# Coupling pass of a graph network kernel: radial part beside the vector part in a 57 column message, sums over four tiles at once

## The chip, the cores and the metric

The kernel runs on one core of a Trainium2 chip (trn2). The metric is the device time of one execution in microseconds. The engines of the core are TensorE (PE in the profile; PEld is its weight load), VectorE (DVE), ScalarE (ACT), GpSimd (POOL) and SyncE (SP); each works through its own instruction stream in order, and they meet at semaphores.

## The reference, cut to what matters

The reference applies four graph layers to 12,500 nodes of 32 values and 400,000 edges, with a residual and a layer norm after each. The change touches the third layer only, a coupling with spherical harmonics. Its features are 8 scalars and 8 vectors of 3 components:

```python
R = jax.nn.relu(abs_distances[:, None] @ w1 + b1) @ w2 + b2      # (E, 384)
Y = spherical_harmonics(rel_vec)
Fj = features[src]
for i, (mo, lo) in enumerate(RS):                # RS = [(8, 0), (8, 1)]
    acc = jnp.zeros((E, mo, 2 * lo + 1))
    for j, (mi, li) in enumerate(RS):
        ...
        acc = acc + _NORM[i] * jnp.einsum('euv,ef,evi,ofi->euo', Rb[..., k], Yf, Fb, C)
    msg_blocks.append(acc.reshape(E, -1))
msg = jnp.concatenate(msg_blocks, axis=-1)       # (E, 32)
out = out.at[dst].add(msg)
```

The edges are sorted by `dst`. The coupling is worked out in the kernel as 40 sums of 16 terms for each edge: 8 for the scalar part of the message, 8 for a coefficient that multiplies the unit vector of the edge (the radial part), and 24 for the vector part. The vector output of an edge is the vector part plus the unit vector times its coefficient.

## The kernel before, in words

**Tiles and steps.** The edges, padded to groups, lie in tiles of 128, one edge on each partition. A step takes 8 tiles (`TPS`), in four groups of two tiles (`GPS`, `TILES_PER_GROUP`); the edges of a group go to nodes of one window of 128. The coupling pass has 416 steps: 104 iterations (`ITERS`) of 4 slots (`SLOTS`).

**What each engine does for step n** (all `radial_...` functions):

- GpSimd (`radial_gather`): 8 indirect DMAs fetch the features of the source nodes (L779). Three tensor operations, the "geometry" (L819, L820, L824), make the cross products for a later step; they stand between the first four and the last four gathers. In 96 of the 104 iterations (`LATE_ROUNDS`, 384 steps) two further indirect DMAs (L760) fetch edge records that only the last iterations will use: the late records.
- ScalarE (`radial_round`) copies unit vectors and features into place (L1077 to L1082), applies the bias and relu to the hidden layer (L1088), makes the one-hot matrices that select a node (L1094, L1099), and copies the sums of each group back into the accumulator (`keep_sums`, L1057).
- TensorE (`radial_step`, L1396) makes for each pair p = 0 to 3 of tiles two matmuls of 384 columns, the radial weights (L1405), called R0 to R3 below. They go to banks 1 and 2 for even p and to 3 and 4 for odd p. Between them stand the hidden layer of the next step (L1371, L1377) and the four group sums of the step before (`radial_sums`: L1390 loads the accumulator, L1392 adds two tiles). The order is fixed: R0, L1371, R1, sums 0, R2, half of the hidden layer, sums 1, R3, sums 2, the other half, sums 3.
- VectorE (`radial_step`, L2453) multiplies the radial weights of pair p by the features into `prod` (L2467 for the first 256 columns of both tiles, L2472 for the rest of each tile) and sums 16 terms at a time into `red` (L2478).

**Semaphores around the change.** `r_ready` tells VectorE that the pair's matmuls are done; `r_used`, raised by the second L2472 of pair p, lets TensorE overwrite the banks two pairs later: R2 waits for pair 0, R3 for pair 1, R0 of the next step for pair 2, R1 for pair 3. `hid_ready` (ScalarE) gates R0 as well. `msg_ready`, raised by L2485, lets TensorE start sums 0 of that step and ScalarE start its copies for the step after the next. `geo_ops` makes VectorE wait for the geometry of GpSimd, `geo_ready` makes GpSimd wait for the copies of ScalarE.

**The end of a step on VectorE.** After the four sums L2481 forms the radial part (24 columns) in a tile of its own, and L2485 adds it to columns 16 to 39 of `red`. Then L2457 and L2461 start the next step.

`prod` has two halves, each of two tiles, so pair p overwrites what pair p-2 left. The names `C2` (41), `red`, `radial` and `prod` are those that the change touches.

## Time and profile before

| what | value |
|---|---|
| median of 3 runs | 20600.07 us (20592.81 to 20604.26) |
| the profiled execution's own time | 20595.7 us |
| its span, first to last instruction | 20593.9 us |
| coupling pass in the span, first to last multiplication and sum of VectorE | 10738.7 to 16783.6 us |
| VectorE busy over the span | 17281.9 us (84%) |
| GpSimd busy over the span | 13246.4 us (64%) |
| TensorE matmul busy over the span | 9779.6 us (47%) |
| mean granted TensorE clock | 0.67 |

The time is that of the whole execution; the span lies 1.8 us below it. The passes follow each other with little overlap, so a change within the coupling pass is to be read from the rows of that pass. Rows of one timeline give the start, the duration, engine, line, operation, the tiles written and read, the count merged into the row, and in brackets the idle time before it with what ended it.

### The profile page before, as it was taken

The page shows a single profiled execution, that of the slowest core. Times are in us where ns is not written, and L with a number is a line of the kernel's source. Part 1 is how long each engine was busy: PE and PEld are TensorE (multiplying, and loading weights), DVE is VectorE, ACT ScalarE, POOL GpSimd, SP SyncE. Part 2 cuts the span into 40 slices and gives each one's busy share as a digit, 9 for nine tenths or more (in the row PEclk, how much of TensorE's full clock was granted, in tenths as well). Part 3 has the DMA queues.
Part 4 walks back from the last instruction along what each step waited for, and adds up shares of the span by engine and source line. Part 5 has one row for each costly group of instructions (what it writes and reads, how often), then busy time and mean ns, then how long its engine had stood idle before and what let it go on. Part 6 is the DMA issues. An engine that isn't in the chain of part 4 may idle for free.

```text
span 20593.9 us, 293981 instructions
## 1 busy us (share of the span) xinstructions
PE 9779.6 (47%) x63545; PEld 7463.1 (36%) x63546; DVE 17281.9 (84%) x25284; ACT 5966.3 (29%) x13901; POOL 13246.4 (64%) x14067
## 2 busy tenths in 40 slices
PE   0114010110016777653348777777777765336432
PEld 0114010100015666643235555555555544225322
DVE  9989999999997888787659999999999986664666
ACT  0000333333322222230004444454545445004300
POOL 0058777777777777735757777777777731770376
PEclk9655555555558888755558888888888875555555
DMA  1033444444412112174331111111111147336534
GB/s 18 0 54 24 30 35 31 33 31 32 33 22 45 36 36 36 34 242 124 84 52 12 12 12 12 12 12 12 12 12 12 12 89 230 79 77 162 181 79 68
DMA packets 1751558, 1095.98 MB, mean 53 GB/s; under 512 B 1217323, under 2 KB 1658124, under 8 KB 1750028
## 3 DMA queue, kind: packets, MB, share of 16 engines
q0 software_dynamic: 454272, 412.11, 18.2%
q1 hardware_dynamic: 1089532, 417.46, 8.2%
q10 hardware_dynamic: 207632, 265.14, 4.1%
q14 instruction: 88, 0.72, 0.0%
q8 instruction: 34, 0.56, 0.0%
HBM read 700.94 MB, written 391.12 MB: 53 GB/s over the span
## 4 chain that ended last, share of the span: by engine, by line
DVE 43%; DVEq 20%; issue 12%; DMA 10%; PE 10%; POOL 3%; ACT 1%; ACTq 0%; POOLq 0%; SPq 0%
DVEq L2477 11%; DMA srcs<-spread,nbx 9%; DVE arena L1750 7%; DVE arena L1749 6%; DVE srcs L2472 6%; POOL srcs L801 3%; DVE red L2478 3%; PE banks L1264 2%; DVEq L2205 2%; PE banks L1347 2%; DVE arena L1722 2%; DVE arena L2173 2%; DVE arena L1567 2%; PE banks L1405 1%; PE banks L1193 1%
## 5 line engine op out<-in xcount | busy, mean ns | idle before, releaser
L779 POOL DMA_INDIRECT gat<-tab,nbr x3328 | 3509.4, 1054 | 2151.3 <-DMA nbr<-nbr_src 1137.2
L801 POOL DMA_INDIRECT srcs<-spread,nbx x2808 | 2654.9, 945 | 2713.5 <-DMA nbx<-from_src 1375.3
L779 POOL DMA_INDIRECT gat<-tab,pay x3328 | 3176.8, 955 | 1078.4 <-issue 854.3
L1405 PE MATMUL banks<-w2rows,dsts 128*128 128x384 f32 x6656 | 3177.9, 613 | 894.1 <-DVE srcs L2472 700.2
L745 POOL DMA_INDIRECT pay<-records,nbr x2560 | 2489.7, 973 | 797.7 <-issue 780.0
L2478 DVE TENSOR_REDUCE red<-srcs 128x80 f32<-128x1280 f32 x1664 | 2474.6, 1487 | 151.4
L2173 DVE TENSOR_TENSOR arena<-arena,banks 128x96 f32 (+2 forms) x4472 | 1210.4, 271 | 1474.0 <-PE banks L1264 890.6
L1193 PE MATMUL banks<-ident,arena 128*128 128x128 f32 x2240 | 426.3, 376 | 4231.5 <-DVE arena L1750 2810.2
L1264 PE MATMUL banks<-srcs,hot 128*128 128x96 bf16 (+1 forms) x11232 | 1148.5, 278 | 2482.7 <-DMA srcs<-spread,nbx 2364.0
L906 ACT COPY banks<-arena 128x1024 f32<-128x1024 f32 (+1 forms) x1508 | 1324.5, 879 | 3299.6 <-DVE arena L1750 1275.6
L1405 PEld LDWEIGHTS banks<-w2rows,dsts 128*128 128x128 f32 x6656 | 1359.9, 227 | 1735.0 <-DVE srcs L2472 849.2
L1193 PEld LDWEIGHTS banks<-ident,arena 128*128 128x128 f32 x2240 | 401.4, 203 | 4257.7 <-DVE arena L1750 2820.3
L1264 PEld LDWEIGHTS banks<-srcs,hot 128*128 128x128 bf16 x11232 | 883.1, 135 | 2748.1 <-issue 1567.9
L2472 DVE TENSOR_TENSOR srcs<-banks,g_v 128x384 f32<-128x384 f32 x3328 | 1685.0, 548 | 0.0
L1749 DVE TENSOR_TENSOR arena<-banks,arena 128x1024 f32<-128x1024 f32 (+1 forms) x1508 | 1544.0, 1024 | 22.8 <-ACT banks L906 22.8
L1750 DVE TENSOR_TENSOR arena<-banks,arena 128x1024 f32<-128x1024 f32 (+1 forms) x1508 | 1544.1, 1024 | 0.0
L1347 PE MATMUL banks<-arena,hotT 128*128 x11232 | 1078.8, 282 | 829.8 <-DVE hotT L2260 576.6
L2260 DVE TENSOR_SCALAR hotT<-dsts,lanes 128x1024 bf16<-128x1024 uint8 x1404 | 1026.8, 757 | 469.5 <-PE banks L1347 467.1
L1347 PEld LDWEIGHTS banks<-arena,hotT 128*128 128x128 bf16 x11232 | 894.4, 141 | 1014.0 <-issue 1009.6
L2467 DVE TENSOR_TENSOR srcs<-banks,g_s 128x512 f32<-128x512 f32 x1664 | 1137.6, 684 | 142.1 <-issue 96.6
L2162 DVE TENSOR_TENSOR hot<-banks,key_dst 128x1024 bf16<-128x1024 f32 x936 | 1141.4, 1220 | 53.1 <-issue 52.9
L1392 PE MATMUL banks<-red,hot 128*128 128x41 f32 x6656 | 1162.5, 307 | 0.0
(394 smaller groups left out, 20741.4 us busy)
## 6 DMA issues: line engine op xcount, KB each, us to landing
spread<-srcs SPq DMA_DIRECT2D x936, 192.0 KB
dsts<-key_rows SPq DMA_DIRECT2D x234, 512.0 KB, 4.1
spread<-srcs ACTq DMA_DIRECT2D x468, 204.0 KB
staged<-gat SPq DMA_DIRECT2D x416, 148.0 KB, 1.8
gat<-staged ACTq DMA_DIRECT2D x416, 148.0 KB
dsts<-key_rows ACTq DMA_DIRECT2D x117, 512.0 KB, 4.5
gat<-tab,nbr POOLq DMA_INDIRECT x3328
gat<-tab,pay POOLq DMA_INDIRECT x3328
```

The lines of the kernel that those rows point to most:

```text
L745: pool.indirect_dma_start(out=pay[:, s, t, :], out_offset=None, in_=records, in_offset=bass.IndirectOffsetOnAxis(ap=nbr[:, s, t:t + 1], ax ...
L779: pool.indirect_dma_start(out=gatv(s, GC[pas])[:, t, :], out_offset=None, in_=TAB[pas], in_offset=bass.IndirectOffsetOnAxis(ap=row, axis=0 ...
L801: pool.indirect_dma_start(out=chunk_rows(s, c)[:, q, :], out_offset=None, in_=rows, in_offset=bass.IndirectOffsetOnAxis(ap=nbx[:, r, s * X ...
L1264: last = t_.matmul(where(q), hots[:, t, :], rows(t), start=(h == 0), stop=(h == tiles - 1))
L1347: last = t_.matmul(bank[2 * (s % 2) + q][:, j * c3:(j + 1) * c3], hotT_row[s % 2][:, q * XGROUP + j:(q + 1) * XGROUP:CHUNK_EDGES], tabs[:, ...
L1405: last = t_.matmul(bank[1 + 2 * (p % 2) + h][:, 0:384], hid_rows[:, s % 2, 2 * p + h, :], w2rows[:, :], start=True, stop=True)
L1749: v.tensor_tensor(b[:, d, e, :, :, :], held, a[:, d, 1, :, :, :], ALU.min)
L1750: last = v.tensor_tensor(b[:, d, 1 - e, :, :, :], held, a[:, d, 1, :, :, :], ALU.max)
L2173: last = v.tensor_tensor(dst, dst, where(q), ALU.add)
L2472: last = v.tensor_tensor(prod[:, pb, h, 16:40, :].rearrange("p (u o) k -> p u o k", o=3), bank[lo + h][:, 256:384].rearrange("p (u a k) -> ...
L2477: dve.drain()
L2478: v.tensor_reduce(red[:, b, t0:t0 + 2, 0:40], prod[:, pb, :, :, :], AX.X, ALU.add)
```

## The change

Each message gets 57 columns in place of 41. `red` is 65 columns wide: 0 to 7 hold the radial coefficients, 8 to 15 the scalar part, 16 to 39 the vector part, 40 a one that counts the edges, and 41 to 64 the radial part. TensorE sends columns 8 to 64. The radial part is written there directly and is no longer added on VectorE; it is added once, per node, after the pass. `prod` is one buffer of four tiles, and the sum over 16 terms is taken after every second pair, over four tiles. The two blocks of `w2rows` are swapped to match, and the late records of GpSimd stay as they were.

```diff
-C2 = 41
+C2 = 57
+CR = 65
...
-        red = sb("red", [P, 2, TPS, C2])
+        red = sb("red", [P, 2, TPS, CR])
...
-        prod = srcs[:, 0:4 * 640].bitcast(F32).rearrange("p (b t r k) -> p b t r k", b=2, t=2, k=16)
+        prod = srcs[:, 0:4 * 640].bitcast(F32).rearrange("p (t r k) -> p t r k", t=TPS // 2, k=16)
...
-        radial = sb("radial", [P, TPS, 24])
...
-                    last = t_.matmul(where, hot[:, s % 2, t, :], red[:, s % 2, t, :], start=False,
+                    last = t_.matmul(where, hot[:, s % 2, t, :], red[:, s % 2, t, 8:CR], start=False,
...
-                    t0, pb, lo = 2 * p, p % 2, 1 + 2 * (p % 2)
+                    t0, f0, lo = 2 * p, 2 * (p % 2), 1 + 2 * (p % 2)
                     dve.wait_ge(r_ready, n * (TPS // 2) + (p + 1))
-                    v.tensor_tensor(prod[:, pb, :, 0:16, :],
+                    v.tensor_tensor(prod[:, f0:f0 + 2, 0:16, :],
...
                     last.then_inc(r_used, 1)
-                    dve.drain()
-                    v.tensor_reduce(red[:, b, t0:t0 + 2, 0:40], prod[:, pb, :, :, :], AX.X, ALU.add)
-                dve.drain()
-
-                v.tensor_tensor(radial[:, :, :].rearrange("p t (u o) -> p t u o", o=3),
+                    if p % 2:
+                        dve.drain()
+                        v.tensor_reduce(red[:, b, t0 - 2:t0 + 2, 0:40], prod[:, :, :, :], AX.X, ALU.add)
+                        dve.drain()
+
+                v.tensor_tensor(red[:, b, :, 41:CR].rearrange("p t (u o) -> p t u o", o=3),
                                 rx[:, b, :, 0:3].rearrange("p t (a o) -> p t a o", a=1).to_broadcast([P, TPS, 8, 3]),
-                                red[:, b, :, 8:16].rearrange("p t (u a) -> p t u a", a=1).to_broadcast([P, TPS, 8, 3]), ALU.mult)
-                dve.drain()
-                v.tensor_tensor(red[:, b, :, 16:40], red[:, b, :, 16:40], radial[:, :, :], ALU.add).then_inc(msg_ready, 1)
+                                red[:, b, :, 0:8].rearrange("p t (u a) -> p t u a", a=1).to_broadcast([P, TPS, 8, 3]),
+                                ALU.mult).then_inc(msg_ready, 1)
...
-            v.tensor_tensor(x[:, :, 8:F], x[:, :, 8:F], a2[:, :, 16:40], ALU.add)
-            v.tensor_copy(dinv[:, :], a2[:, :, 40])
+            v.tensor_tensor(x[:, :, 8:F], x[:, :, 8:F], a2[:, :, 8:F], ALU.add)
+            v.tensor_copy(dinv[:, :], a2[:, :, F])
+            dve.drain()
+            v.tensor_tensor(x[:, :, 8:F], x[:, :, 8:F], a2[:, :, F + 1:C2], ALU.add)
```

On VectorE, one step of the coupling pass from its first product to that of the next step, before the change (`srcs` holds `prod`, `banks` the radial weights, `dsts` the hidden layer):

```order
5405 L2467 TENSOR_TENSOR srcs<-banks,g_s 128x2x256
5406 L2472 TENSOR_TENSOR srcs<-banks,g_v 128x384 x2
5407 L2478 TENSOR_REDUCE red<-srcs 128x2x40
5408 L2467 TENSOR_TENSOR srcs<-banks,g_s 128x2x256
5409 L2472 TENSOR_TENSOR srcs<-banks,g_v 128x384 x2
5410 L2478 TENSOR_REDUCE red<-srcs 128x2x40
5411 L2467 TENSOR_TENSOR srcs<-banks,g_s 128x2x256
5412 L2472 TENSOR_TENSOR srcs<-banks,g_v 128x384 x2
5413 L2478 TENSOR_REDUCE red<-srcs 128x2x40
```

The fourth pair follows in the same way, then L2481 and L2485. The same place after the change, with the end of the step:

```order
5405 L2467 TENSOR_TENSOR srcs<-banks,g_s 128x2x256
5406 L2472 TENSOR_TENSOR srcs<-banks,g_v 128x384 x2
5407 L2467 TENSOR_TENSOR srcs<-banks,g_s 128x2x256
5408 L2472 TENSOR_TENSOR srcs<-banks,g_v 128x384 x2
5409 L2479 TENSOR_REDUCE red<-srcs 128x4x40
5410 L2467 TENSOR_TENSOR srcs<-banks,g_s 128x2x256
5411 L2472 TENSOR_TENSOR srcs<-banks,g_v 128x384 x2
5412 L2467 TENSOR_TENSOR srcs<-banks,g_s 128x2x256
5413 L2472 TENSOR_TENSOR srcs<-banks,g_v 128x384 x2
5414 L2479 TENSOR_REDUCE red<-srcs 128x4x40
5415 L2482 TENSOR_TENSOR red<-rx,red 128x8x24
```

The products of two pairs now stand next to each other, with the sum behind the second, and the step has two sums and one operation on the radial part, where it had four sums and two operations. TensorE, ScalarE and GpSimd keep their order; on TensorE the sums have 57 columns, and so have the copies of ScalarE.

## Rows read from the trace of the kernel before

**Rows 1.** Windows: length, busy (instructions) of PE, PEld, DVE, ACT, POOL; clock, DMA, GB/s.
```profile
11100.00:12200.00 1100.00, 859.95 (x3721) 569.01 (x3720) 1025.83 (x1515) 545.94 (x1742) 843.84 (x986) 0.85 0.10 12
16312.00:16783.00 471.00, 364.03 (x1584) 242.20 (x1583) 439.84 (x649) 228.63 (x730) 282.56 (x338) 0.85 0.30 10
```

**Rows 2.** Groups by line, VectorE, 11000 to 16200 us: busy, mean ns | idle before.
```profile
L2478 DVE TENSOR_REDUCE red<-srcs 128x80 f32<-128x1280 f32 x1434 | 2132.5, 1487 | 130.5
...
L2485 DVE TENSOR_TENSOR red<-red,radial 128x192 f32<-128x192 f32 x358 | 130.2, 364 | 26.8
...
L2461 DVE TENSOR_REDUCE g_s<-tmpC 128x64 f32<-128x192 f32 x358 | 126.3, 353 | 26.2
```

**Rows 3.** Timeline, VectorE, one step: start, us, engine, line, operation, [idle before].
```profile
12027.50 0.69 DVE L2467 TENSOR_TENSOR srcs<-banks,g_s 128x512 f32<-128x512 f32 x1 [0.34 <-issue]
12028.11 1.01 DVE L2472 TENSOR_TENSOR srcs<-banks,g_v 128x384 f32<-128x384 f32 x2
12029.21 1.49 DVE L2478 TENSOR_REDUCE red<-srcs 128x80 f32<-128x1280 f32 x1
12030.62 0.68 DVE L2467 TENSOR_TENSOR srcs<-banks,g_s 128x512 f32<-128x512 f32 x1
...
12038.53 1.49 DVE L2478 TENSOR_REDUCE red<-srcs 128x80 f32<-128x1280 f32 x1
12040.09 0.36 DVE L2481 TENSOR_TENSOR radial<-rx,red 128x192 f32<-128x192 f32 x1
12040.52 0.36 DVE L2485 TENSOR_TENSOR red<-red,radial 128x192 f32<-128x192 f32 x1
12040.79 0.37 DVE L2457 TENSOR_TENSOR tmpC<-fT,rx 128x192 f32<-128x192 f32 x1
12041.23 0.35 DVE L2461 TENSOR_REDUCE g_s<-tmpC 128x64 f32<-128x192 f32 x1
12042.43 0.69 DVE L2467 TENSOR_TENSOR srcs<-banks,g_s 128x512 f32<-128x512 f32 x1 [0.84 <-PE banks L1405]
```

**Rows 4.** Groups by line, GpSimd, the same stretch: the first geometry operation.
```profile
L819 POOL TENSOR_TENSOR tmpA<-fT,rx 128x192 f32<-128x192 f32 x358 | 190.8, 533 | 125.6 <-ACT fT L1080 121.1
```

**Rows 5.** Timeline, GpSimd, one step with late records in which it never waits.
```profile
10761.90 0.95 POOL L779 DMA_INDIRECT gat<-tab,pay  x1 [0.30 <-issue]
...
10766.62 0.53 POOL L819 TENSOR_TENSOR tmpA<-fT,rx 128x192 f32<-128x192 f32 x1
...
10773.54 0.94 POOL L760 DMA_INDIRECT late<-records,nbr  x1 [0.30 <-issue]
...
10776.04 0.94 POOL L779 DMA_INDIRECT gat<-tab,pay  x1 [0.30 <-issue]
```

**Rows 6.** Timeline, TensorE, around the same step as rows 3, and a later R3.
```profile
12023.69 1.56 PE L1405 MATMUL banks<-w2rows,dsts 128*128 128x384 f32 x4
12026.52 0.41 PE L1390 MATMUL banks<-arena,ident 128*128 x2 [1.27 <-DVE red L2485]
12026.76 0.62 PE L1392 MATMUL banks<-red,hot 128*128 128x41 f32 x4
12029.18 2.93 PE L1405 MATMUL banks<-w2rows,dsts 128*128 128x384 f32 x4 [1.80 <-DVE srcs L2472]
...
12033.57 2.91 PE L1405 MATMUL banks<-w2rows,dsts 128*128 128x384 f32 x4
...
12042.29 2.87 PE L1405 MATMUL banks<-w2rows,dsts 128*128 128x384 f32 x4
...
14077.92 2.91 PE L1405 MATMUL banks<-w2rows,dsts 128*128 128x384 f32 x4
```

**Rows 7.** Window of 10 us that holds R2 and R3 of rows 6: columns as in rows 1.
```profile
12029.00:12039.00 10.00, 9.69 (x32) 6.88 (x33) 9.64 (x14) 1.31 (x4) 7.88 (x10) 0.50 0.08 9
```

**Rows 8.** Groups by line, TensorE, whole span: sums of 41 columns, and of 133 elsewhere.
```profile
L1392 PE MATMUL banks<-red,hot 128*128 128x41 f32 x6656 | 1162.5, 307 | 0.0
...
L1264 PE MATMUL banks<-msg,hot 128*128 128x133 f32 x3328 | 508.9, 314 | 24.4 <-DVE msg L2221 15.0
```

More of the change, by code:

```diff
@@ L2031, in _ @@
             w2tv = w2t[:, :].rearrange("p (u v) -> p u v", v=8)
-            v.tensor_scalar(q_[:, 0:8, 0:8], blk[0], cp["s_f0"], None, ALU.mult)
-            v.tensor_scalar(q_[:, 0:8, 8:16], blk[1], cp["s_dot"], None, ALU.mult)
-            v.tensor_scalar(q_[:, 8:16, 0:8], blk[2], cp["v_f0"], None, ALU.mult)
-            v.tensor_scalar(q_[:, 8:16, 8:16], vec[:, :, :, 2], 3.0 * cp["v_quad"], None, ALU.mult)
+            v.tensor_scalar(q_[:, 8:16, 0:8], blk[0], cp["s_f0"], None, ALU.mult)
+            v.tensor_scalar(q_[:, 8:16, 8:16], blk[1], cp["s_dot"], None, ALU.mult)
+            v.tensor_scalar(q_[:, 0:8, 0:8], blk[2], cp["v_f0"], None, ALU.mult)
+            v.tensor_scalar(q_[:, 0:8, 8:16], vec[:, :, :, 2], 3.0 * cp["v_quad"], None, ALU.mult)
             v.tensor_scalar(ab[:, :, 8:16], vec[:, :, :, 1], cp["v_cross"], None, ALU.mult)
```

2 lines of the change are left out of this document (1 added, 1 removed).

## The prediction

> **What bounds the kernel now.** The change lives in one stage, so I read the windows of that stage first, then VectorE's groups and one step of its timeline, then the timelines of the two engines that would be next, GpSimd and TensorE.
>
> In 1100 us of the steady pass VectorE is busy 1025.83 us, 93%, with 1515 instructions [rows 1]. A step has 20 of them, so the stretch holds 75.8 steps of 14.50 us. The last 471 us, with no late records, hold 649 instructions, also 14.5 us a step. So the two indirect DMAs of the late records do not set the pace now; VectorE does. Most of its idle time is the short gap before an operation that follows a drain: 130.5 us over 1434 sums, 0.09 us each [rows 2]. The reader should see that VectorE runs almost without waiting, and that GpSimd is close behind: in a step in which it waited for nothing it went from its first gather to that of the next step in 10776.04 - 10761.90 = 14.14 us [rows 5]. Its wait for ScalarE's copies is 121.1 us over 358 steps, 0.34 us each [rows 4], and 14.50 - 0.34 = 14.16 us: the same floor from the other side.
>
> **What the change takes from VectorE.** From starts to starts [rows 3]:
> - A sum of 1280 terms takes 1487 ns, one of 192 terms 353 ns [rows 2]. Over 1088 terms that is 1134 ns, 1.042 ns a term, and 153 ns fixed. A sum of 2560 terms is then 1487 + 1280 x 1.042 = 2.82 us.
> - A pair before: product to sum 1.71 us (12027.50 to 12029.21), sum to next product 1.41 us; the last sum has a drain behind it and takes 1.56 us (12038.53 to 12040.09).
> - After: in the first pair of two no drain follows the product. The two L2472 end at 12029.12 and the sum starts 0.09 us later; a product that follows without a drain starts about as much before the end as it does behind the sum (1.49 us long, next start after 1.41), 0.08 us. So this pair takes 1.71 - 0.17 = 1.54 us, the second 1.71 us, and the long sum with its drain 1.56 + 1.33 = 2.89 us: 6.14 us for half a step.
> - Four pairs before: 4 x 1.71 + 3 x 1.41 + 1.56 = 12.63 us. After: 2 x 6.14 = 12.28 us. Gain 0.35 us. It is this small because the terms stay the same; only two fixed parts and two exposed drains go, and a drain comes in behind the first sum.
> - L2485 goes: from 12040.09 to 12040.52, 0.43 us. L2482 writes strided columns, as L2485 did, and costs what L2481 did (0.36 us).
>
> Together 0.78 us: VectorE alone would do a step in 13.72 us.
>
> **What it adds elsewhere.** TensorE sends 57 columns instead of 41. A sum of 133 columns takes 314 ns where one of 41 takes 307 [rows 8], so 16 columns cost between 0 and 16/92 of 7 ns, 1 ns; I take nothing. ScalarE's copies, four a step, hang behind these sums; TensorE waits for them only between sums and has idle time, so I take nothing there too. After the pass one more addition of 2352 values and a longer clearing before it (1568 more): at 1.042 ns a value about 4 us, once.
>
> **What is late next.** Two engines compete.
>
> GpSimd: 384 of the 416 steps carry late records and cannot go below 14.14 to 14.16 us. VectorE would then wait at `geo_ops`. Saved there: 14.50 - 14.16 = 0.34 us, 131 us in all. In the other 32 steps GpSimd has two DMAs less (10776.04 - 10773.54 = 2.5 us) and does not bind: 32 x 0.78 = 25 us. Less 4 us this gives 152 us, the most that this kernel can gain unless GpSimd gets faster.
>
> TensorE: the change moves the time at which R3 is needed. Counted from a step's first product, pair 3 starts before at 3 x 3.11 = 9.33 us, after at 6.14 + 1.54 = 7.68 us. R2 cannot start before `r_used` of pair 0, 12029.18 - 12027.50 = 1.68 us in both kernels. At the full clock R2 and R3 take 1.56 us each [rows 6], and R3 ends at about 6.4 us: on time. But TensorE idles at the turn of a step, 1.27 us before sums 0 and 1.80 us before R2 [rows 6], and then the granted clock drops to 0.50, the level of 1.2 GHz, for 10 us [rows 7]. There R2 and R3 take 2.93 and 2.91 us, and R3 ends at 12036.48, 8.98 us after the first product: in time before, 1.3 us late after. R1 of the next step ended at 12045.16, and VectorE would have wanted it about 1.2 us earlier. In 127 steps between 12000 and 14100 us that I followed, R3 ended over 0.1 us later than the new time in 30 (the first and last are 12033.57 and 14077.92 [rows 6]), by 0.15 to 1.35 us; spread over all steps 0.15 us, and R1 behind them 0.14 us more.
>
> So at the present share of slow stretches (mean clock 0.85 [rows 1], so 0.30 of the time at half) TensorE adds 0.29 us to 13.72: 14.01 us, below GpSimd's floor. The share will rise: `r_used` of pair 3 comes earlier relative to `msg_ready` (a sum of 2.89 us stands between, before 1.56), so R1 ends earlier and the idle time before sums 0 grows by some 0.6 us. Bounds: none of it (14.01) and every step late by 1.35 us (15.07). I take twice the present price, 0.58 us, 14.30 us, because only one step in four was late before and the idle stretch grows by a fifth of 3.1 us. The slips partly fall into the time in which VectorE would wait for GpSimd anyway, so I set a late step at 14.28 us.
>
> The profile shows that idle stretches of 1.3 and 1.8 us are followed by the low clock. The Trainium skill, TensorE: Matmul & The Clock Gate, section HAM oscillation, says the same of loops that starve TensorE: it slows after each wait, "every single K-tile". By that rule alone every step would start slow and the sum would be a loss; here 97 of 127 steps did not make R3 late, so the rule is taken as a rival and not as the forecast.
>
> **The sum.** 384 x (14.50 - 14.28) = 84 us, 32 x 0.22 = 7 us (there TensorE alone binds), less 4 us: 87 us. The profiled execution took 20595.7 us, 1.8 us of it outside the span, so 20508.7; the median lies 4.4 us above that execution: 20513 us.
>
> **Rivals.**
> 1. GpSimd is the only new bound: gain 152 us, 20448 us. For it: 14.01 is below 14.16, and GpSimd's waits for ScalarE should vanish once it is the slowest. Against: the clock.
> 2. The clock eats nearly everything: TensorE's price is about 0.7 us (2.5 times the present one), a step takes 14.41 us or more, and the time stays within 0.2% (41 us), about what a measurement of this kernel can tell from no change. 20580 us.
> 3. Slower: every step starts with the low clock, R3 late by 1.35 us each time. A step is 13.72 + 1.35 = 15.07 us, 416 x 0.57 = 237 us more: 20841 us. It decides once the mean lateness of a step passes 0.88 us (14.6 us a step). For it: both idle stretches lie in every step. Against: a late R3 leaves TensorE no idle time behind it, and after such a stretch (12042.29 [rows 6]) it has caught up; so not every step can be hit. Half of it, 14.8 us, gives 20725 us.
> 4. GpSimd does not bind, VectorE alone counts: 416 x 0.78 - 4 = 320 us, 20280 us. It needs GpSimd's 14.14 us to shrink, and nothing in the change shortens an instruction there.
>
> **How the numbers follow.** Forecast, a late step between 14.20 and 14.37 us: 0.45, own range 20479 to 20550. Rival 1: 0.24. Rival 2: 0.16. Rival 3: 0.12. Rival 4: 0.03. Faster by over 0.2% (below 20559) is the forecast, rivals 1 and 4: 0.72, cut to 0.70. Within 0.2%: 0.17. Slower: 0.13. The range goes from just below rival 1, 20438, over rival 2 to 20620, a part of rival 3; outside it lie rival 4 and most of rival 3.
>
> **What would show it.** The sum L2479 at 2.82 us, 832 of them, two a step; no second operation behind L2482, and the matmuls of L1392 with 57 columns still at about 307 ns. If GpSimd binds, its wait for ScalarE at L819 falls from 121.1 us to near nothing and VectorE shows idle time before L2467 that GpSimd ends. If TensorE binds, VectorE waits for L1405 before the products of pair 3 and pair 1, and the granted clock of the pass falls below 0.85. A long sum well over 2.9 us, or a clock that rises, would make the prediction wrong, as would a floor of GpSimd other than 14.14 us.

## The result: 0.8% faster, the whole of what GpSimd allows

The changed kernel takes 20428.38 us (median of 4 runs, 20417.71 to 20433.55), the kernel before 20599.65 us beside it (4 runs, 20592.81 to 20604.26): a ratio of 0.9916, 95% interval 0.9899 to 0.9934, or 171 us less. The forecast was 87 us less. The sign was right; the size was that of the first rival (152 us) and a little over, and the time lies 10 us below the low end of the range. The profiled execution took 20431.26 us with a span of 20429.5 us.

Windows of the kernel after, with the columns of [rows 1]: the same 1100 us, and the end of the pass, where no late records are left.

```profile
11100.00:12200.00 1100.00, 838.47 (x3814) 558.52 (x3813) 1011.65 (x1324) 565.01 (x1792) 863.18 (x1011) 0.89 0.09 12
16200.00:16640.00 440.00, 349.70 (x1514) 233.23 (x1512) 403.09 (x529) 218.58 (x697) 271.96 (x326) 0.83 0.28 11
```

A step of VectorE has 17 instructions now, so the first stretch holds 1324 / 17 = 77.9 steps of 14.12 us, where it held 75.8 before. GpSimd executes 1011 instructions instead of 986. And the granted clock is 0.89, not 0.85.

The first and the last start of one line give the mean step over the whole pass. Line of the kernel after that names VectorE's first geometry operation, 416 times: shortest, median and longest in ns, first and last start in us.

```profile
L2457 DVE TENSOR_TENSOR tmpC<-fT,rx x416: 359/367/418, 10746.5 to 16623.6; 128x192 f32<-128x192 f32 x139
```

That is (16623.6 - 10746.5) / 415 = 14.162 us a step; before, the same two starts lay at 10738.7 and 16769.6, 14.532 us. The late steps alone (first to last DMA of L760, less the 1.25 us between the two of a step, over 383) went from 14.507 to 14.160 us. From the first L2457 to the first operation behind the pass the time fell from 6053.5 to 5899.1 us, by 154 us. The other 10 us of the profiled difference lie outside it: 8 us longer ahead of this pass and 18 us shorter behind it. Of these the change itself accounts only for 3.9 us more, the longer clearing ahead (4.71 us instead of 3.41) and the addition behind (2.61 us); nothing forecast the rest.

Groups by line of the kernel after, 11000 to 16000 us: busy, mean ns | idle time before, and what ended it.

```profile
L2479 DVE TENSOR_REDUCE red<-srcs 128x160 f32<-128x2560 f32 x706 | 1990.8, 2820 | 64.3
...
L2467 DVE TENSOR_TENSOR srcs<-banks,g_s 128x512 f32<-128x512 f32 x1413 | 971.2, 687 | 278.0 <-PE banks L1405 156.1 <-issue 71.4
...
L1392 PE MATMUL banks<-red,hot 128*128 128x57 f32 x5656 | 937.9, 292 | 0.0
...
L1390 PE MATMUL banks<-arena,ident 128*128 x2828 | 588.3, 292 | 612.0 <-ACT arena L1057 473.1 <-DVE red L2482 122.5 <-issue 12.7
...
L819 POOL TENSOR_TENSOR tmpA<-fT,rx 128x192 f32<-128x192 f32 x354 | 189.6, 536 | 6.2
...
L1077 ACT COPY rx<-pay 128x24 f32<-128x24 f32 x353 | 76.3, 216 | 1088.5 <-DMA gat<-tab,pay 1088.3
```

The reader should see four things. The long sum takes 2820 ns, as worked out ahead. A sum of 57 columns takes 292 ns, so the 16 further columns cost nothing that shows [rows 8]. GpSimd was idle before L819 for 122.1 us in this stretch before the change, 117.8 of them waiting for ScalarE, and for 6.2 us now. And ScalarE's first copy of a step, which waited for VectorE before (141.9 of its 142.6 us), now waits 1088.3 us for the gathers, 3.1 us in each step. The chain of work that ended last, over the whole span, tells the same: GpSimd had 3% of it before.

```profile
DVE 32%; POOL 21%; issue 15%; DMA 11%; DVEq 9%; PE 8%; ACT 2%; ACTq 1%; POOLq 0%; SPq 0%
```

So GpSimd sets the pace. One step of the kernel after in the timelines of all four engines shows how it reaches the others. GpSimd first:

```profile
12001.88 0.95 POOL L779 DMA_INDIRECT gat<-tab,pay  x1 [0.30 <-issue]
...
12012.26 0.94 POOL L779 DMA_INDIRECT gat<-tab,pay  x1 [0.30 <-issue]
...
12016.00 0.94 POOL L779 DMA_INDIRECT gat<-tab,pay  x1 [0.30 <-issue]
...
12030.15 0.94 POOL L779 DMA_INDIRECT gat<-tab,pay  x1 [0.30 <-ACT fT L1080]
```

It goes round in 14.12 and 14.15 us, the wait-free step of [rows 5]. The eighth gather of a step is issued at 12012.26. ScalarE:

```profile
12014.66 0.22 ACT L1077 COPY rx<-pay 128x24 f32<-128x24 f32 x1 [3.87 <-DMA gat<-tab,pay]
...
12015.24 0.36 ACT L1080 COPY fT<-gat 128x128 f32<-128x128 f32 x1
...
12016.00 0.20 ACT L1057 COPY arena<-banks 128x57 f32 x1
```

Its six copies (L1077 to L1082) start when the gathers have landed, and stand ahead of L1057, which keeps the sums 0 of the message. TensorE, from R2 to the next sums 0:

```profile
12012.16 1.56 PE L1405 MATMUL banks<-w2rows,dsts 128*128 128x384 f32 x4 [1.52 <-DVE srcs L2472]
...
12016.44 0.42 PE L1390 MATMUL banks<-arena,ident 128*128 x2 [2.50 <-ACT arena L1057]
...
12017.15 1.51 PE L1405 MATMUL banks<-w2rows,dsts 128*128 128x384 f32 x4
...
12022.60 1.51 PE L1405 MATMUL banks<-w2rows,dsts 128*128 128x384 f32 x4
12023.94 0.39 PE L1390 MATMUL banks<-arena,ident 128*128 x2
```

The sums 1 wait 2.50 us for that L1057, and R3, which stands behind them in program order, starts at 12017.15, although R2 had ended at 12013.72 and VectorE had read pair 1 at 12013.63. VectorE then waits for it, before pair 3:

```profile
12016.69 0.69 DVE L2467 TENSOR_TENSOR srcs<-banks,g_s 128x512 f32<-128x512 f32 x1
...
12018.70 0.69 DVE L2467 TENSOR_TENSOR srcs<-banks,g_s 128x512 f32<-128x512 f32 x1 [0.40 <-PE banks L1405]
```

The wait that VectorE shows is called TensorE's, and its source is GpSimd, three engines back. In this step there is also no idle time left between R1 and the sums 0 (12022.60, 12023.94), where 1.27 us stood in the step of [rows 6]. Over 11000 to 16000 us the mean of that idle time fell from 0.73 to 0.36 us; I expected it to grow by 0.6 us, and the clock to fall.

### The profile page after: what moved, and what is told of

It is laid out like the page before. It is cut to its first block, busy times and chain, and to the rows that moved or that the text cites. A ratio compares the mean times of both kernels' runs of the same rounds, so it can differ in the third digit from the quotient of the medians.

```text
span 20429.5 us, 291903 instructions
## 1 busy us (share of the span) xinstructions
PE 9564.9 (47%) x63545; PEld 7338.7 (36%) x63546; DVE 17060.7 (84%) x24037; ACT 5987.8 (29%) x13901; POOL 13233.3 (65%) x14067
## 4 chain that ended last, share of the span: by engine, by line
DVE 32%; POOL 21%; issue 15%; DMA 11%; DVEq 9%; PE 8%; ACT 2%; ACTq 1%; POOLq 0%; SPq 0%
POOL gat L779 12%; DMA srcs<-spread,nbx 9%; DVE arena L1750 7%; DVE arena L1749 6%; POOL srcs L801 3%; PE banks L1264 3%; POOL late L760 2%; DVEq L2205 2%; PE banks L1347 2%; DVE arena L1722 2%; DVE arena L2173 2%; DVE arena L1567 2%; PE banks L1193 1%; DVE hotT L2260 1%; DMA gat<-tab,pay 1%
## 5 line engine op out<-in xcount | busy, mean ns | idle before, releaser
L1405 PE MATMUL banks<-w2rows,dsts 128*128 128x384 f32 x6656 | 2991.6, 586 | 688.2 <-DVE srcs L2472 557.7
L2479 DVE TENSOR_REDUCE red<-srcs 128x160 f32<-128x2560 f32 x832 | 2346.1, 2820 | 75.8
L1405 PEld LDWEIGHTS banks<-w2rows,dsts 128*128 128x128 f32 x6656 | 1305.0, 218 | 1447.9 <-DVE srcs L2472 649.8
L1392 PE MATMUL banks<-red,hot 128*128 128x57 f32 x6656 | 1107.3, 293 | 0.0
```

The source lines that it names most:

```text
L1405: last = t_.matmul(bank[1 + 2 * (p % 2) + h][:, 0:384], hid_rows[:, s % 2, 2 * p + h, :], w2rows[:, :], start=True, stop=True)
L2479: v.tensor_reduce(red[:, b, t0 - 2:t0 + 2, 0:40], prod[:, :, :, :], AX.X, ALU.add)
```

## The experiments

Two readings of the result stood against each other (the expectations call them theory G and theory T): GpSimd sets the pace, and what TensorE is late lies in its shadow; or the step is VectorE's work plus TensorE's lateness, only smaller than forecast. Eight runs fell on chips where the kernel before takes 20600 us; they carry the explanation. The mean step of each is from the first and last start of VectorE's first geometry operation, as above; it holds the 32 steps without late records too.

| kernel | ratio to before, 95% interval | mean step, us | VectorE's wait for TensorE, 11000 to 16000 us |
|---|---|---|---|
| before | 1 | 14.532 | 28.7 us |
| after | 0.9916 (0.9899 to 0.9934) | 14.162 | 156.1 us |
| e3b: 57 columns alone | 0.9918 (0.9902 to 0.9935) | 14.160 | 86.3 us |
| e4b: four-tile sums alone | 0.9995 (0.9986 to 1.0005) | 14.567 | 112.4 us |
| e2b: before, no late records | 0.9992 (0.9982 to 1.0001) | 14.551 | 45.2 us |
| e1b: after, no late records | 0.9903 (0.9887 to 0.9920) | 14.081 | 125.4 us |
| e8: 57 columns, two-tile sums, no late records | 0.9888 (0.9872 to 0.9905) | 14.018 | 24.5 us |
| e9: after, no late records, R3 first | 0.9835 (0.9818 to 0.9851) | 13.763 | 45.9 us |
| e5: after, one more operation on GpSimd | 1.0020 (1.0011 to 1.0030) | 14.664 | 334.2 us |
| e11: after, R3 first, two operations in one | 0.9910 (0.9893 to 0.9926) | 14.127 | 168.4 us |

In the kernels without late records the late gathers are issued in the first iteration alone; the last 24 iterations of the pass work on the records that these left.

### GpSimd taken out of both kernels: e1b and e2b

```diff
-                        sp.wait_ge(rec_in[s], i * (16 * LATE_TILES) + 16 * TPS * EARLY_ITERS)
+                        sp.wait_ge(rec_in[s], 16 * LATE_TILES + 16 * TPS * EARLY_ITERS)
...
-                    if late_load:
+                    if late_load and first:
...
             def late_records(i, s, first):
+                if not first:
+                    return
                 pool.wait_ge(nbr_in[s], nbr_count(1, EARLY_ITERS + i))
-                if not first:
-                    pool.wait_ge(rec_out[s], i * 16 + 16 * EARLY_ITERS)
```

This takes two indirect DMAs, 2.5 us, from each of GpSimd's steps.

> The changed kernel without the late gathers of GpSimd in the coupling pass, except in the first iteration, on another chip than before: the first one (26240 us for the kernel before) stalled every engine for several us at a time. SyncE stores the records of the first iteration each time, so the last 24 iterations work on wrong edge records. Theory G (GpSimd alone sets the changed kernel's pace, 14.16 us a step, and hides the price of TensorE): the step falls to VectorE's pace with TensorE's slips, 13.7 to 14.0 us, 60 to 180 us less than the changed kernel. Theory T (TensorE with its clock already sets the pace): the step stays at 14.1 to 14.2 us.

> The kernel before with the same work left out (late gathers only in the first iteration). Both theories: VectorE sets its pace at 14.50 us a step, so the time stays within 20 us of the kernel before. More than 40 us less would mean that GpSimd had a part in its pace.

Measured: 20587.57 us for the kernel before without late records, 22 us less than the 20609.28 us of the kernel before beside it, with an interval that holds 1; 20405.77 us for the changed kernel without them, 203 us less. So 2.5 us a step off GpSimd gave the kernel before nothing that can be told from no change: it had slack. The changed kernel came out some 30 us lower than with them, with intervals that overlap; the profiled steps, 14.081 against 14.162 us, differ the same way. That misses the expectation: theory G asked for 13.7 to 14.0 us and 60 us less at the least, and by the step alone theory T (14.1 to 14.2 us) fits as well. What tells them apart is who waits, here, and what more work on GpSimd costs (e5 below). Groups by line of the changed kernel without late records, same stretch and columns as above:

```profile
L2467 DVE TENSOR_TENSOR srcs<-banks,g_s 128x512 f32<-128x512 f32 x1421 | 976.8, 687 | 255.0 <-PE banks L1405 125.4 <-issue 77.8
...
L819 POOL TENSOR_TENSOR tmpA<-fT,rx 128x192 f32<-128x192 f32 x356 | 186.9, 525 | 880.9 <-ACT fT L1080 880.1
```

GpSimd waits 2.5 us a step, so it is out of the way, and what is left is VectorE and TensorE: 14.081 us, of which 125.4 us / 355 = 0.35 us a step are VectorE's wait for L1405. 14.08 less 0.35 is 13.73 us, VectorE's own work; the steps in which no product waited for L1405 average 13.72 us, and the prediction had 13.72. This kernel isolates the term that the prediction had to guess, TensorE's price: 0.35 us, not 0.58. And 14.08 lies under GpSimd's 14.15. That is why the floor of GpSimd showed and nothing else did.

Where the 0.35 us come from can be read step by step. Of e1b, TensorE and then VectorE, in a step whose first product starts at 12025.98:

```profile
12025.26 0.47 PE L1390 MATMUL banks<-arena,ident 128*128 x2 [1.98 <-DVE red L2482]
...
12027.65 2.93 PE L1405 MATMUL banks<-w2rows,dsts 128*128 128x384 f32 x4 [1.06 <-DVE srcs L2472]
...
12032.07 2.88 PE L1405 MATMUL banks<-w2rows,dsts 128*128 128x384 f32 x4
```

```profile
12034.99 0.69 DVE L2467 TENSOR_TENSOR srcs<-banks,g_s 128x512 f32<-128x512 f32 x1 [1.19 <-PE banks L1405]
...
12043.00 0.69 DVE L2467 TENSOR_TENSOR srcs<-banks,g_s 128x512 f32<-128x512 f32 x1 [0.19 <-PE banks L1405]
```

R2 and R3 run at half the clock, with half of the hidden layer and sums 1 between them, and R3 ends 8.97 us after the first product: the 8.98 us of the prediction, 1.19 us too late. Between 11000 and 16000 us this happens in 89 of 355 steps, with R2 and R3 slow in every one of them; in the other 266 R3 takes the full clock and is never late. That is 0.30 us a step before pair 3. Before pair 1 of the next step it is 0.02 us. The sums 1 waited for ScalarE in none of these steps. The idle time before the sums 0 rose from 0.73 us in the kernel before to 0.93 us, and the clock of the pass fell from 0.85 to 0.83.

### Each half of the change alone: e3b and e4b

e3b has the radial part beside the vector part in 57 columns, and still sums over two tiles; e4b sums over four tiles and still sends 41 columns, with the addition on VectorE in place. Both edits are shown against the kernel before.

```diff
 e3b (57 columns alone)
-C2 = 41
+C2 = 57
+CR = 65
...
-                    last = t_.matmul(where, hot[:, s % 2, t, :], red[:, s % 2, t, :], start=False,
+                    last = t_.matmul(where, hot[:, s % 2, t, :], red[:, s % 2, t, 8:CR], start=False,
...
-                dve.drain()
-                v.tensor_tensor(red[:, b, :, 16:40], red[:, b, :, 16:40], radial[:, :, :], ALU.add).then_inc(msg_ready, 1)
 e4b (four-tile sums alone)
-                    dve.drain()
-                    v.tensor_reduce(red[:, b, t0:t0 + 2, 0:40], prod[:, pb, :, :, :], AX.X, ALU.add)
-                dve.drain()
+                    if p % 2:
+                        dve.drain()
+                        v.tensor_reduce(red[:, b, t0 - 2:t0 + 2, 0:40], prod[:, :, :, :], AX.X, ALU.add)
+                        dve.drain()
```

> One part alone: the 57 column message, sums over two tiles as before. VectorE's own step is 14.50 - 0.43 = 14.07 us, just under GpSimd's 14.16. Theory G: a step of 14.16 to 14.2 us, 120 to 155 us faster than before, nearly the whole effect. Theory V (the gains of VectorE add up by their shares): 0.43 of 0.78, 55% of 171, about 95 us.

> The other part alone: sums over four tiles, 41 columns. VectorE's own step is 14.50 - 0.35 = 14.15 us, with R3 wanted at 7.7 us. Theory G with no price for TensorE: 14.16 to 14.2 us, 115 to 140 us faster than before. If TensorE's slips add to VectorE's step, as the prediction had it: 14.45 us or more, and no gain.

Measured: the 57 columns alone gave 20434.73 us against 20609.28, 175 us less, the whole effect of the change. Theory G had 120 to 155 us for that. The four-tile sums alone gave 20594.71 us, 15 us less, with an interval that holds no change: of the two expectations, the one in which TensorE's slips add to VectorE's step. Rows of e3b and then of e4b, by line, 11000 to 16000 us:

```profile
L2467 DVE TENSOR_TENSOR srcs<-banks,g_s 128x512 f32<-128x512 f32 x1412 | 965.5, 684 | 152.0 <-PE banks L1405 86.3 <-issue 64.8
...
L819 POOL TENSOR_TENSOR tmpA<-fT,rx 128x192 f32<-128x192 f32 x353 | 189.2, 536 | 6.0
```

```profile
L2467 DVE TENSOR_TENSOR srcs<-banks,g_s 128x512 f32<-128x512 f32 x1376 | 944.7, 687 | 256.6 <-PE banks L1405 112.4 <-issue 106.4
...
L819 POOL TENSOR_TENSOR tmpA<-fT,rx 128x192 f32<-128x192 f32 x344 | 183.4, 533 | 142.8 <-ACT fT L1080 138.5
```

The columns bring VectorE's step to about 14.0 us, already under GpSimd's floor: L819 no longer waits. For a second gain there is no room. The four-tile sums take 0.25 us from VectorE (its steps without a wait for L1405 average 14.46 us before and 14.22 in e4b) and give it back: its wait for L1405 rose from 28.7 to 112.4 us, 0.24 us a step. R3 came late in 90 of 344 steps, by 1.18 us each, with R2 and R3 at half the clock each time; in the kernel before R3 is as often slow (88 of 344 steps) and never late. The profiled step came out 0.03 us longer and the timed runs 15 us shorter; neither can be told from none. The four-tile sums bring pair 3 forward to about 7.7 us after the first product, and in a slow stretch R3 does not come sooner for it.

### The same halves with GpSimd out of the way: e8

e8 is e3b with the late records left out, as in e1b; against e1b it differs in the four-tile sums alone.

> The 57 column message with sums over two tiles, without late gathers after the first iteration (last 24 iterations on wrong edge records). R3 is wanted at 9.3 us here. VectorE's step is 14.07 us, TensorE's price as in the kernel before (under 0.1 us): 14.1 us, 170 to 210 us less than the kernel before, the same as with sums over four tiles (203 us less), so that the four tile sums are worth nothing even without GpSimd's floor. If the four tile sums had kept their 0.35 us, this kernel would be 100 us or more slower than that one.

Measured: 20379.70 us, 234 us less than the 20614.13 us of the kernel before beside it, where e1b was 203 us less; a step of 14.018 us against 14.081. That is more than the 170 to 210 us expected. With GpSimd out of the way, too, the four-tile sums do not pay: by one profiled step each they cost 0.06 us, and the intervals of the timed runs overlap. The waits say by what:

```profile
L2467 DVE TENSOR_TENSOR srcs<-banks,g_s 128x512 f32<-128x512 f32 x1428 | 976.1, 684 | 101.4 <-issue 76.9 <-PE banks L1405 24.5
```

24.5 us of waiting for L1405 with sums over two tiles (clock 0.90 in the window 11100 to 12200 us), 125.4 us with sums over four (0.83). In e8 R3 is slow in 42 of 357 steps and late in none.

### R3 ahead of the sums: e9

```diff
-                    if more and p == 2:
-                        hidden(n + 1, 0)
-                    if not first and p > 0:
-                        radial_sums(n - 1, (s - 1) % SLOTS, p - 1, wins[p - 1])
+                    if not first and p == 1:
+                        radial_sums(n - 1, (s - 1) % SLOTS, 0, wins[0])
+                    if more and p == 3:
+                        hidden(n + 1, 0)
+                    if not first and p == 3:
+                        radial_sums(n - 1, (s - 1) % SLOTS, 1, wins[1])
+                        radial_sums(n - 1, (s - 1) % SLOTS, 2, wins[2])
```

On TensorE R3 now follows directly on R2; half of the hidden layer and the sums 1 come behind it. Late records are left out as in e1b.

> The changed kernel without late gathers after the first iteration (last 24 iterations on wrong edge records), and on TensorE R3 directly behind R2: half of the hidden layer and sums 1 come after R3 instead of before it. Theory L (TensorE's price of 0.36 us a step in the changed kernel without late gathers, 14.08 against VectorE's 13.72, is R3 arriving late behind sums 1): the price goes, the step falls to 13.7 to 13.85 us, 95 to 160 us less than with the old order (20406 us). Theory C (it is the clock as such, all matmuls slower): the order changes nothing, 14.05 to 14.1 us.

Measured: 20272.90 us, 341 us less than the kernel before and 138 us more gain than e1b. Of e9, the wait and the 416 starts:

```profile
L2470 DVE TENSOR_TENSOR srcs<-banks,g_s 128x512 f32<-128x512 f32 x1456 | 998.7, 686 | 153.0 <-issue 55.4 <-PE banks L1405 45.9
```

```profile
L2460 DVE TENSOR_TENSOR tmpC<-fT,rx x416: 360/368/423, 10732.1 to 16443.8; 128x192 f32<-128x192 f32 x139
```

The step is (16443.8 - 10732.1) / 415 = 13.763 us. This is VectorE's own work, 13.72 us by the prediction's sum and by the steps without a wait for L1405, with 0.04 us on top. The 45.9 us of waiting stand before the first product of a step, where 0.25 us of idle time stand in every step of every kernel here; before pair 3 there is none.

This does not make the clock innocent. L1405 took 616 ns on the mean here and 613 in e1b, but the slow matmuls are other ones: in e9 R2 and R3 ran at the full clock in 354 of 364 steps, and R0 was slow in 318. The ten steps in which R2 and R3 were slow show what the order alone does. One of them, TensorE and VectorE, with the first product at 12293.27:

```profile
12294.95 5.49 PE L1405 MATMUL banks<-w2rows,dsts 128*128 128x384 f32 x8 [1.52 <-DVE srcs L2475]
```

```profile
12301.01 0.68 DVE L2470 TENSOR_TENSOR srcs<-banks,g_s 128x512 f32<-128x512 f32 x1
```

R2 and R3 together take 5.49 us and end 7.17 us after the first product, in time. So TensorE's price needs two things at once: the low clock in R2 and R3, and work in the queue between them. Taking either away removes it: the work in these ten steps of e9, the low clock in the 266 steps of e1b. That the clock of R2 and R3 itself rose with the new order is seen here; why, no run separates.

### GpSimd given more to do: e5

```diff
+                    g.tensor_tensor(tmpD[:, :, :].rearrange("p t (o v) -> p t o v", o=3), tA, tB, ALU.subtract)
                     g.tensor_tensor(g_v[:, b, :, :, 8:16], tA, tB, ALU.subtract).then_inc(geo_ops, 1)
```

> The changed kernel with one more tensor operation of GpSimd in each step (the subtraction of the geometry, done twice; 0.6 to 0.75 us). Theory G (GpSimd sets the pace): the late steps grow by the whole operation, 384 x 0.6 to 0.75 = 230 to 290 us, and the time passes that of the kernel before. If another engine set the pace, GpSimd's wait-free step would only reach 14.8 us and the time would grow by 0 to 100 us.

Measured: 20653.10 us, 39 us above the kernel before, and so some 210 us above the changed kernel; 230 to 290 us were expected, from a longer operation. Timeline of GpSimd in e5, and its first geometry operation by line:

```profile
12008.06 0.53 POOL L820 TENSOR_TENSOR tmpA<-fT,rx 128x192 f32<-128x192 f32 x1
...
12009.21 0.59 POOL L825 TENSOR_TENSOR tmpD<-tmpA,tmpB 128x192 f32<-128x192 f32 x1
12009.75 0.59 POOL L826 TENSOR_TENSOR g_v<-tmpA,tmpB 128x192 f32<-128x192 f32 x1
```

```profile
L820 POOL TENSOR_TENSOR tmpA<-fT,rx 128x192 f32<-128x192 f32 x340 | 182.4, 536 | 5.6
```

The operation takes 0.54 us from start to start, and the late step grew from 14.160 to 14.707 us: all of it. An operation added to an engine with slack costs nothing; here it cost its full length in each of 384 steps, 0.55 x 384 = 210 us. GpSimd has no slack left in the changed kernel.

### Both reliefs while GpSimd binds: e11

e11 is the changed kernel with R3 first, as in e9, with the late records in place, and with the two multiplications of the geometry made one:

```diff
-                    g.tensor_tensor(tA, fT[:, b, :, 2:5, :], r_(b, 1), ALU.mult).then_inc(geo_ops, 1)
-                    g.tensor_tensor(tB, fT[:, b, :, 1:4, :], r_(b, 2), ALU.mult).then_inc(geo_ops, 1)
+                    g.tensor_tensor(tmpAB[:, :, :, :], both(fT[:, b, :, 2:5, :], -8), both(rx[:, b, :, 1:4, :], 8),
+                                    ALU.mult).then_inc(geo_ops, 2)
```

> A candidate: the changed kernel with R3 directly behind R2 on TensorE, and the two multiplications of GpSimd's geometry in one operation of twice the size (ScalarE writes the unit vectors eight times over for it, about 0.4 us more a step there). If a GpSimd operation has a fixed part of 0.1 to 0.3 us, GpSimd's step falls from 14.14 to 13.85 to 14.05 us, and with R3 no longer late the whole step follows: 35 to 110 us less than the changed kernel. If the operation is all per element, nothing is gained.

Measured: 20423.80 us against 20614.13, 190 us less where the changed kernel was 171 us less, a ratio of 0.9910 where it has 0.9916. By line:

```profile
L2470 DVE TENSOR_TENSOR srcs<-banks,g_s 128x512 f32<-128x512 f32 x1413 | 971.1, 687 | 262.0 <-PE banks L1405 168.4 <-issue 54.9
...
L819 POOL TENSOR_TENSOR tmpAB<-fT,rx 128x384 f32<-128x384 f32 x353 | 357.1, 1012 | 5.9
...
L824 POOL TENSOR_TENSOR g_v<-tmpAB 128x192 f32<-128x192 f32 x353 | 208.9, 592 | 50.6
```

The merged operation takes 1012 ns where the two took 536 and 530. Even that difference is not gained: the two overlap, and from the start of the first to the start of L824 it is 1.16 us in both kernels. So GpSimd's late step stayed what it was, 14.15 us, and moving R3, worth 138 us in e9, was worth 20 us at most here (the intervals overlap). The same order of R3 with and without GpSimd's floor shows that the lateness of TensorE is not added to GpSimd's time; it disappears under it. e11 also gives ScalarE more to write; the order alone with the late records in place ran only as e10, on the other kind of chip below.

### Ten runs on other chips

On four other chips every kernel, the kernel before among them, took 25,100 to 26,900 us. The passes that gather run longer there (GpSimd executes 1383 instructions between 2000 and 4000 us, where it executed 1523), the engines show waits for a releaser that the trace does not name, and GpSimd, which never waited in the changed kernel above, waits 1231.1 us / 265, 4.6 us a step, for ScalarE's copies. Waits of the changed kernel there (e12), 16000 to 21000 us: in total, times, longest.

```profile
POOL tmpA L819 <- ACT fT L1080: 1231.1, 207, 12.1
ACT arena L1057 <- remote: 1193.1, 192, 13.7
...
DVE srcs L2467 <- remote: 1013.6, 266, 9.1
```

Its late steps took (21738.0 - 14533.7 - 1.25) / 383 = 18.81 us, well above the wait-free step of GpSimd (14.14 us) and of VectorE (13.72 us). What sets them is open. The expectations had been written for the chips above, and these runs decide none of them:

> The changed kernel without the late gathers of GpSimd in the coupling pass, except in the first iteration (SyncE stores the records of that iteration each time, so the last 24 iterations work on wrong edge records). GpSimd's own step falls from 14.14 to 11.64 us. Theory G (GpSimd alone sets the changed kernel's pace, 14.16 us a step, and hides the price of TensorE): the step falls to the pace of VectorE with TensorE's slips, between 13.72 and 14.0 us, 60 to 180 us less than the changed kernel, and VectorE's waits for R3 show up openly. Theory T (TensorE with its clock already sets the pace, and GpSimd's full occupation is a coincidence): the step stays at 14.1 to 14.2 us, and the time within 20 us of the changed kernel's 20428 us.

> The kernel before with the same work left out (late gathers only in the first iteration). Both theories: VectorE sets its pace at 14.50 us a step, so the time stays within 20 us of the kernel before. A gain of more than 40 us would mean that GpSimd had a part in the pace of the kernel before.

> One part alone: the 57 column message without the addition on VectorE, sums over two tiles as before. VectorE's own step is 14.50 - 0.43 = 14.07 us, just under GpSimd's 14.16. Theory G: a step of 14.16 to 14.2 us, 120 to 155 us faster than before, nearly the whole effect of the change. Theory V (the gains of VectorE add up, each part gives its share): 0.43 of 0.78, so 55% of 171, about 95 us.

> The other part alone: sums over four tiles, 41 columns, the radial part added on VectorE. VectorE's own step is 14.50 - 0.35 = 14.15 us, with R3 wanted at 7.7 us as in the changed kernel. Theory G with no price for TensorE: 14.16 to 14.2 us, 115 to 140 us faster than before. If TensorE's slips add to VectorE's step, as the prediction had it: 14.15 + 0.3 to 0.6, a step of 14.45 us or more, and no gain.

> The changed kernel again, as the point of reference for the three that follow. Both theories: 0.9916 of the kernel before, about 170 us less, GpSimd in 14.14 us per late step without waits, the mean late step 14.16 us.

> The changed kernel with R3 issued on TensorE directly behind R2, ahead of sums 1. Theory G (GpSimd sets the pace of the late steps, the lateness of R3 lies in its slack): the mean late step stays at 14.16 us and the time within 20 us of the changed kernel. Theory T (TensorE's lateness is still paid on top of GpSimd's time, as the prediction's sum has it): the late step falls by up to the whole 0.4 us that R3 is late on the mean, 150 us off the changed kernel's time.

> The changed kernel with R3 directly behind R2, and the subtraction of the geometry for four of the eight tiles moved from GpSimd to VectorE. Theory G: GpSimd's own work falls from 14.14 to about 13.87 us per step, VectorE's rises to about 13.9, and the mean late step comes out at 13.9 to 14.05 us: 40 to 100 us less than the changed kernel. Theory T (the step is VectorE's work plus TensorE's lateness): VectorE has more to do, so the time is no less than that of R3 moved alone and may be 60 us above it.

> The kernel before with one more subtraction of the geometry on GpSimd (0.55 to 0.67 us). Theory G (GpSimd had 0.36 us of slack per late step before): the late step rises from 14.51 to 14.7 to 14.8 us, 75 to 120 us above the kernel before, and not by the whole operation. Rival (GpSimd was as much on the path before as after): the whole 0.55 us shows in each of 384 steps, 210 us.

> The kernel of e13_split_r3 again, on another chip: R3 directly behind R2 on TensorE, and the geometry's subtraction for four of the eight tiles moved from GpSimd to VectorE. Theory G (GpSimd sets the pace of the late steps after the change): GpSimd's own work falls from 14.14 to about 13.87 us per step, VectorE's rises to about 13.9, the mean late step comes out at 13.9 to 14.05 us: a ratio to the kernel before of 0.987 to 0.990, 40 to 100 us better than the changed kernel. Theory T (the step is VectorE's work plus TensorE's lateness): with more work on VectorE the ratio is 0.991 to 0.995.

> The kernel of e13b_split_r3 again, on another chip: R3 directly behind R2 on TensorE, and the geometry's subtraction for four of the eight tiles moved from GpSimd to VectorE. Theory G (GpSimd sets the pace of the late steps after the change): GpSimd's own work falls from 14.14 to about 13.87 us per step, VectorE's rises to about 13.9, the mean late step comes out at 13.9 to 14.05 us: a ratio to the kernel before of 0.987 to 0.990, 40 to 100 us better than the changed kernel. Theory T (the step is VectorE's work plus TensorE's lateness): with more work on VectorE the ratio is 0.991 to 0.995.

| kernel | ratio to before there, 95% interval |
|---|---|
| e12: the changed kernel | 0.9988 (0.9976 to 0.9999) |
| e3: 57 columns alone | 1.0013 (0.9995 to 1.0032) |
| e4: four-tile sums alone | 1.0001 (0.9985 to 1.0016) |
| e1, e2: after and before without late records | 0.9569 (0.9544 to 0.9594), 0.9586 (0.9567 to 0.9605) |
| e10: after, R3 first | 1.0070 (1.0054 to 1.0087) |
| e13, e13b, e13c: R3 first, half of a subtraction moved to VectorE | 1.0083 (1.0050 to 1.0116), 1.0086 (1.0063 to 1.0109), 1.0127 (1.0108 to 1.0145) |
| e6: before, one more operation on GpSimd | 0.9858 (0.9842 to 0.9875) |

The edits of those that are new: e10 is the R3 edit of e9 on the changed kernel, e6 the operation of e5 on the kernel before, and e13 has, beside R3 first,

```diff
-                    g.tensor_tensor(g_v[:, b, :, :, 8:16], tA, tB, ALU.subtract).then_inc(geo_ops, 1)
+                    g.tensor_tensor(g_v[:, b, 0:4, :, 8:16], tA[:, 0:4, :, :], tB[:, 0:4, :, :], ALU.subtract).then_inc(geo_ops, 1)
...
+                v.tensor_tensor(g_v[:, b, 4:8, :, 8:16], tA, tB, ALU.subtract).then_inc(geo_sub, 1)
```

Two things follow all the same. The gain of 0.8% belongs to the chips of the first table; on the one other chip where the changed kernel ran it gained 0.1%. And two edits go there against what an engine's load would say: R3 first, which gained in e9, makes the changed kernel 0.8% slower, and one more operation on GpSimd makes the kernel before 1.4% faster, while the instructions take the same time as ever, such as 2820 ns for the long sum. Only leaving out the late gathers helps more, by 4%. This points at the gathers, not at the engines, but no run separates that. Whether e13 beats both kernels where GpSimd binds, and how much of e5's 0.55 us the kernel before would have absorbed (e6), was asked on those chips alone and stays open.

## Why the prediction was right in sign and wrong in size

**VectorE's bound**: right. The sum of 93% busy steps of 14.50 us was the step, and 2.5 us less on GpSimd (e2b) moved the kernel before by nothing that is told from zero.

**What the change takes from VectorE**: right in the total, off in the halves. 0.78 us were worked out, 13.72 us left. Steps in which no product waited for L1405 average 14.46 us in the kernel before and 13.72 in e1b and e9. But the four-tile sums took 0.25 us of this (e4b against before, e1b against e8), not 0.35, and the addition 0.49 us, not 0.43. One row that the sum had too short is the step from a long sum with its drain to the next product, 2.96 us in e1b (12029.22 to 12032.18) where 2.89 was taken. The long sum itself took 2.82 us as computed from two shorter ones.

**57 columns and the copies at nothing**: right, 292 ns a sum, and e3b with the 57 columns had the full gain.

**GpSimd's floor**: right, 14.16 us twice over. The late step came out at 14.160.

**TensorE's price**: the step that failed. The prediction worked out 0.29 us from the steps that it had followed, 0.15 for R3 and 0.14 for R1 behind it, then wrote "I take twice the present price, 0.58 us". Measured in e1b it is 0.35 us. R3's part doubled as taken, to 0.30 us: one step in four, late by 1.19 us. R1's part did not: it is 0.02 us where 0.28 was taken. The prediction counted one slip twice. It asked when VectorE would have wanted R1 had R3 been in time; but R3's lateness holds VectorE up as well, so that R1, 1.2 us late by that reckoning, stops VectorE for 0.19 us in the step of e1b above.

The reason given for doubling was an idle time before the sums 0 that grows by 0.6 us, and a falling clock. In e1b, where the price can be read, that idle time grew by 0.2 us and the clock fell from 0.85 to 0.83; the share of steps with a slow R3 (over 2.2 us) stayed at one in four, 88 of 344 before and 89 of 355. That R3's part came out at twice 0.15 us all the same is luck, as far as this reason goes. In the changed kernel itself, held back by GpSimd, the idle time halved and the clock of the pass rose to 0.89. The prediction had named a clock that rises as a sign against itself.

With 0.35 in place of 0.58 the sum reads 13.72 + 0.35 = 14.07 us, under GpSimd's 14.16: the floor alone counts, and that is rival 1, 152 us, which stood at a chance of 0.24. The pass lost 154 us. So the wrong size of one term also chose the wrong case, since the two bounds lie only 0.1 us apart. The 17 us between that and the 171 us measured lie outside the pass or in the scatter of the runs.

**The cause given for TensorE's price** holds, with one half unsaid. The prediction followed the low clock: at half speed R3 ends 1.3 us late. So it does, in 89 steps of e1b. The other half is the work that stands between R2 and R3. e9 moved it, and R3 was in time even in ten steps at half the clock.

**How slips add**: the prediction let them "partly fall into the time in which VectorE would wait for GpSimd anyway" and took 0.02 us off for it. Between 14.08 and 14.16 all of it falls there, as e11 against e9 shows.

**The rule on the clock gate** was rightly a rival only. The Trainium skill, TensorE: Matmul & The Clock Gate, section HAM oscillation, has a loop that starves TensorE slow down after each wait; that loop waits longer, for DMA, than TensorE waits here. The traces go both ways. In the changed kernel waits of 1.52 and 2.50 us stand in the step above, with R2 and R3 at 1.56 and 1.51 us, the full clock; in e1b waits of 1.98 and 1.06 us are followed by R2 and R3 at half of it. The third rival, built on the low clock in every step, fell: R3 was slow in one step of four.

**The range** ended 10 us below rival 1, at 20438. The other passes alone moved by 10 us between the two profiled executions, and the median of the kernel before differed by 14 us from chip to chip (20599.65 to 20614.13). A range that is to hold a rival has to hold its scatter.

**The size of the change**: the gain was sought in two parts and came from one. That the four-tile sums give nothing, on either side of the floor, was not in the text; it would nearly have followed from its own numbers, 0.35 us gained against up to 0.29 us of TensorE's price that comes in mostly with these sums, since they are what moves the time of R3 from 9.33 to 7.68 us. Measured, 0.25 us stand against some 0.3.

## What to carry to other kernels

When an engine that sets the pace is eased by more than the slack of the next one, the gain is the slack: work it out from a step in which that engine waited for nothing, and take the maximum of the bounds, not their sum. Before sizing a lateness by a slower clock, ask what stands ahead of the late instruction in its queue: here the lateness needed both, and putting the wanted matmuls ahead of the others removed it. Two slips of one engine in one step are not to be added before asking whether the first also delays the one who waits for the second. An edit that shortens an engine's work but moves forward the time at which it wants its input should be charged for that at once: here the whole 0.25 us was gone.

## What the hardware showed that I had not expected

GpSimd's element-wise operation has no fixed part that merging could save at these sizes: 536 and 530 ns for two of 192 fp32 elements a partition, started 0.48 us apart, 1012 ns for one of 384, and 1.16 us to the operation behind them in either kernel (e11 against after). VectorE's products of 192 elements take 0.36 us. On VectorE merging four sums into two, with 153 ns fixed in each by the prediction's two sizes, took 0.25 us from a step.

The granted clock can fall to half although TensorE is never idle for long: in e1b no idle time of it between 11000 and 16000 us is above 1.98 us, and in 89 of 355 steps R2 and R3 ran at half the clock.

A chip can differ from the next by 27 to 29% on the same kernel, with the same time for instructions such as the long sum (2820 ns on both): 20600 and 26235 to 26639 us for the kernel before. On the second kind R3 first lost and a further operation gained, so a ratio of a few tenths of a per cent holds for the kind of chip on which it was taken.
